# One threshold evaluation of the first attention step moves from VectorE to ScalarE

## The reference, cut to what matters

```
logits = (Xa @ W1) @ W2 @ (Xa @ W3).T
vals   = logits sorted downwards in each row
csum   = cumsum(softmax(vals));  k = sum(csum < 0.9) + 1
A      = softmax(logits with all but the k largest set to -inf)
Xf, Xb, Xa = Rf @ Xf, Rb @ Xb, A @ Xa
Z     += Xf @ U1[s] + Xb @ U2[s] + Xa @ U3[s]
```

## Time and profile before

| what | value |
|---|---|
| median of 3 runs | 2127.34 us (2127.3 to 2127.66) |
| the profiled execution's own time | 2128.81 us |
| its span, first to last instruction | 2127.0 us |
| PE busy | 1859.8 us, 87% of the span |
| DVE busy | 1703.2 us, 80% |
| ACT busy | 1253.2 us, 59% |
| POOL busy | 331.4 us, 16% |
| chain that ended last | DVE 35%, PE 28%, DVE's queue 13%, ACT 13%, issue 10% |

### The profile page before, as it was taken

How to read it: one execution, slowest core, us unless ns; L and a number is a source line. 1 busy time by engine, 2 the same in 40 slices (tenths; PEclk the granted TensorE clock), 3 DMA queues, 4 the chain that set the end, 5 groups by cost and what they waited for, 6 DMA issues and landing times.

```text
span 2127.0 us, 36276 instructions
## 1 busy us (share of the span) xinstructions
PE 1859.8 (87%) x10984; PEld 1378.1 (65%) x10984; DVE 1703.2 (80%) x4231; ACT 1253.2 (59%) x2027; POOL 331.4 (16%) x765
## 2 busy tenths in 40 slices
PE   3999864999999999996846479999999999999997
PEld 2888732777777777775645156666666656666665
DVE  6444557888888888888882489999999999999996
ACT  5222255666666666664521658676777767686752
POOL 4000030000000000000000021313223231313130
PEclk9999967999999999998878689999999999999999
DMA  6899620110111111111003010101101010101022
GB/s 155 200 202 200 169 96 20 47 42 30 42 46 46 46 46 42 30 42 46 22 22 111 5 41 20 40 20 39 34 25 38 21 39 20 39 20 39 20 102 67
DMA packets 60619, 123.87 MB, mean 58 GB/s; under 512 B 13731, under 2 KB 45857, under 8 KB 60448
## 3 DMA queue, kind: packets, MB, share of 16 engines
q1 hardware_dynamic: 50000, 93.58, 13.0%
q0 software_dynamic: 3744, 22.14, 6.8%
q10 hardware_dynamic: 6832, 7.67, 1.0%
HBM read 107.99 MB, written 37.49 MB: 68 GB/s over the span
## 4 chain that ended last, share of the span: by engine, by line
DVE 35%; PE 28%; DVEq 13%; ACT 13%; issue 10%; ACTq 1%; DMA 0%; POOL 0%; POOLq 0%; SPq 0%
DVE scraps L1244 8%; DVE stats L1358 6%; DVE window L1244 5%; PE lg L965 4%; PE bank L1032 3%; PE bank L1011 3%; DVEq L1539 3%; ACT expo L752 3%; ACT turned L771 3%; ACT turned L769 3%; PE bank L986 3%; PE bank L1000 2%; DVE window L1401 2%; DVEq L1405 2%; PE bank L913 2%
## 5 line engine op out<-in xcount | busy, mean ns | idle before, releaser
L1011 PE MATMUL bank<-xcur,probs_t 128*128 128x256 f32 x2704 | 592.2, 379 | 0.0
L1011 PEld LDWEIGHTS bank<-xcur,probs_t 128*128 128x128 f32 x2704 | 509.7, 190 | 67.1
L805 ACT ACTIVATE probs_t<-bank 128x512 f32<-128x512 f32 (+1 forms) x364 | 190.2, 565 | 248.2 <-PE bank L1000 247.0
L1000 PE MATMUL bank<-ident,window 128*128 128x128 f32 x1352 | 200.7, 289 | 131.6 <-DVE kept_inv L1541 117.5
L1000 PEld LDWEIGHTS bank<-ident,window 128*128 128x128 f32 x1352 | 150.4, 145 | 231.2 <-DVE kept_inv L1541 141.3
L986 PE MATMUL bank<-both,s_tile 128*128 128x512 f16 x1352 | 300.1, 379 | 0.0
L1229 DVE TENSOR_SCALAR_CACHE_REDUCE expo<-lg 128x1024 f32 (+1 forms) x208 | 205.0, 1022 | 63.7 <-PE lg L965 53.1
L965 PE MATMUL lg<-k_t,q_tile 64*128 64x512 f32 (+1 forms) x832 | 197.5, 575 | 53.4 <-DVE expo L1229 25.2
L771 ACT ACTIVATE turned<-expo,found 128x3327 uint8<-128x3327 f32 x78 | 239.6, 3072 | 5.3
L769 ACT ACTIVATE turned<-expo,found 128x3327 uint8<-128x3327 f32 x78 | 239.3, 3068 | 3.8
L1358 DVE MAX8 stats<-window 128x8 f32<-128x208 f32 (+1 forms) x780 | 238.8, 384 | 0.0
(11 more groups left out here) (265 smaller groups left out, 2602.0 us busy)
## 6 DMA issues: line engine op xcount, KB each, us to landing
s_tile<-s_scratch SPq DMA_DIRECT2D x52, 832.0 KB, 4.5
expo<-in_adj POOLq DMA_DIRECT2D x25, 831.8 KB, 9.9
s_scratch<-s_tile SPq DMA_DIRECT2D x14, 832.0 KB, 9.5
s_scratch<-probs_t SPq DMA_DIRECT2D x6, 832.0 KB, 9.9
s_scratch<-window SPq DMA_DIRECT2D x6, 832.0 KB, 9.9
q_tile<-q_scratch SPq DMA_DIRECT2D x104, 32.0 KB, 2.1
xa_scratch<-ht ACTq DMA_DIRECT2D x26, 128.0 KB, 1.7
y_scratch<-y_tile SPq DMA_DIRECT2D x26, 128.0 KB, 1.7
```

Source lines behind the costliest of these rows:

```text
L805: A.activation(probs_t[:, k0 * P:(k0 + n) * P], flip_ps[g % 2][:, 0:n * P], ACT.Copy).then_inc(p_moved[s], 1)
L1000: last = T.transpose(flip_ps[g % 2][:, k * P:(k + 1) * P], window[:, (k0 + k) * P:(k0 + k + 1) * P], ident[:, :])
L1011: last = T.matmul(pv_ps[:, 0:D], probs_t[:, k * P:(k + 1) * P], xcur[:, k, :], start=(k == 0), stop=(k == NT - 1))
```

## The change

The constant that says how many evaluations ACT makes in the first attention step goes from 1 to 2. `refine(b, 1)`, which stands behind the scaling of `ht` in ACT's step, now runs there too, and makes the evaluation and the power step that DVE's `evaluate` made. ACT's first evaluation of the first attention step reads only every second column of `expo`, 1664 of 3327, and its constants are adapted to half the mass. DVE takes the final threshold from a new slot of `found` and goes on with `few`. The second attention step computes what it did.

```diff
-UNDER_LEAST = 0x3A831000
-EVALS_SCALAR = (1, 2)
+EVALS_SCALAR = (2, 2)
...
                     A.activation(bias[:, :], slack[b].bitcast(I32), ACT.Copy, scale=SCALAR_POWER[s],
-                                 bias=SCALAR_POWER[s] * (SCALAR_AIM[s] * BITS - 256.0 * BITS))
+                                 bias=SCALAR_POWER[s] * ((SCALAR_AIM[s] - (1 - s)) * BITS - 256.0 * BITS))
...
                 def refine(b, r):
 
-                    if r >= EVALS_SCALAR[s]:
-                        return
-                    A.activation(unused, expo[b][:, 0:N], ACT.Sign, scale=-1.0, bias=tried[b][r], accum_out=signs[:, :])
+                    every = 2 if s == 0 and r == 0 else 1
+                    seen, sample = unused[:, 0:-(-N // every)], expo[b][:, 0:N:every]
+                    A.activation(seen, sample, ACT.Sign, scale=-1.0, bias=tried[b][r], accum_out=signs[:, :])
+                    if s == 0 and r == 1:
+                        A.activation(goal_at[:, :], tried[b][1], ACT.Identity, scale=AIM[0] + GUARD, bias=slack[b])
                     act.drain()
-                    A.activation(unused, expo[b][:, 0:N], ACT.Relu, scale=-1.0, bias=tried[b][r], accum_out=lack[:, :])
-                    A.activation(neg_count[:, :], signs[:, :], ACT.Copy, scale=-0.5, bias=-N / 2.0 - GUARD)
+                    A.activation(seen, sample, ACT.Relu, scale=-1.0, bias=tried[b][r], accum_out=lack[:, :])
+                    A.activation(neg_count[:, :], signs[:, :], ACT.Copy, scale=-0.5, bias=-(-(-N // every)) / 2.0 - GUARD / every)
+                    if s == 0 and r == 1:
+                        A.activation(last_bias[:, :], goal_at.bitcast(I32), ACT.Copy, scale=POWER, bias=-POWER * 256.0 * BITS)
                     act.drain()
...
-                    A.activation(step_by[:, :], minus_under[b][r].bitcast(I32), ACT.Identity, scale=-SCALAR_POWER[s], bias=bias[:, :])
+                    power, by, after = (POWER, last_bias, last_cut[b]) if r == 1 else (SCALAR_POWER[s], bias, tried[b][1])
+                    A.activation(step_by[:, :], minus_under[b][r].bitcast(I32), ACT.Identity, scale=-power, bias=by[:, :])
                     act.drain()
-                    last = A.activation(tried[b][r + 1].bitcast(I32), tried[b][r].bitcast(I32), ACT.Identity, bias=step_by[:, :])
-                    if s == 0:
+                    last = A.activation(after.bitcast(I32), tried[b][r].bitcast(I32), ACT.Identity, bias=step_by[:, :])
+                    if r == 1:
                         last.then_inc(expo_ready[0], 1)
                     act.drain()
...
                     mass_under(b, terms)
                     dve.drain()
-                    if s == 0:
-                        V.scalar_tensor_tensor(out=weight[:, :], in0=under[:, :].bitcast(I32), scalar=float(UNDER_LEAST),
-                                               in1=goal.bitcast(I32), op0=ALU.max, op1=ALU.subtract)
-                        dve.drain()
-                        V.scalar_tensor_tensor(out=cut.bitcast(I32), in0=weight[:, :], scalar=-POWER, in1=cut.bitcast(I32),
-                                               op0=ALU.mult, op1=ALU.add)
-                        dve.drain()
-                        return
...
                     if s == 0:
                         dve.wait_ge(expo_ready[0], t + 1)
-                        V.tensor_copy(cut, found_of(b, 2, 3))
+                        V.tensor_copy(cut, found_of(b, 7, 8))
...
-                    evaluate(b)
                     if s == 1:
+                        evaluate(b)
                         settle(b)
```

More of the change, by code:

```diff
@@ L170, in graph_layers @@
         slack = [found[:, b, 6:7] for b in range(2)]
+        last_cut = [found[:, b, 7:8] for b in range(2)]
         acts = sb("acts", [P, 8])
@@ L177, in graph_layers @@
         neg_count = acts[:, 4:5]
+        goal_at = acts[:, 5:6]
         step_by = acts[:, 6:7]
+        last_bias = acts[:, 7:8]
         mine = sb("mine", [P, 12])
```

## The result

The change makes the kernel slower: 2226.06 us median (2221.2 to 2230.3, 4 runs) against 2127.32 (2127.19 to 2127.66, 4 runs), ratio 1.0463, 95% interval 1.0438 to 1.0489. The forecast was 2210, with 2180 to 2246 as its range. The profiled execution has a span of 2227.3 us, 100.3 more than the one before. The four runs of the changed kernel lie in two pairs, 2229 and 2230 us at a mean granted clock of 0.936 and 2221 and 2223 us at 0.944; the profiled one is of the first pair.

A forecast was written before the change was run, and what follows sets the result against it. A cycle of waits through PE, DVE and ACT bounds the kernel. First step +5.3, 21 periods +84.4, tile 22's retry back to +82.0, next period +86.9, tile 24's retry +83.4: +83 us on 2127.3, 2210 us; range 2180 to 2246.

The forecast's parts named there:

- DVE out of the ring: First attention step: DVE, relieved of 4.38 us per tile, leaves the one-period cycle of waits through PE, DVE and ACT.
- The exponential at S+8.0: ACT's exponential starts 8.0 us after S, the start of a period's timeline, in place of 11.3.
- The halved evaluation hidden: ACT's first evaluation on 1664 columns ends at S+16.9, before the result of A @ Xa at S+18.5: 1.6 us spare.
- Rival C: The stride eats the halving's gain: 1.3 us on 23 periods, +30, 2240 us; chance 0.08.
- The second evaluation, 7.96 us: ACT, between `ht` and the copies PE waits for: a full evaluation's 7.66 us plus two 128 x 1 activations.
- The period without the clock, 31.7: First attention step: 31.7 us per period against 28.68 if PE's clock does not fall behind its new 3.7 us wait.
- The retries: Tiles 22 and 24 retry as before; the first ends at S(22)+19.2, so the shift falls by 7.7 us.
- B: Worse thresholds from the halved first evaluation change retries: two more, 2248 us (chance 0.19); one fewer, 2191 (0.07).
- The prologue and the first step: Before the loop ACT's first threshold comes 5.0 us later, DVE saves 4.38: +0.7; with the first step, +5.3.
- S(1): Start of step 1, forecast at 395.5 against 390.22: +5.3 us.
- The clock, 1.0 us per period: Behind PE's new 3.7 us wait the clock can fall to 0.50; cost 0 to 1.9 us, taken as 1.0.
- S(22): Start of step 22, 21 periods of 32.7 us after S(1) against 28.68: +84.4, together +89.7.

The follow-up runs named there:

- the filled wait: Changed kernel with 29 matmuls of 256 columns without use in PE's wait before the keys and queries; 2192.58 us.
- the halved one: Kernel before with only ACT's first evaluation of the first attention step reading every second column; 2106.99 us, ratio 0.9909.
- the split one: Changed kernel with ACT's second evaluation cut into three pieces placed elsewhere in ACT's step; 2135.10 us, ratio 1.0035 to the kernel before.

## Why the prediction was right, and by how much it was short

The order of the steps as the prediction had them:

- **DVE out of the ring**: right. It waits for the first logits 10.4 us per tile (0.94 before); `few` no longer decides anything.
- **The exponential at S+8.0**: right, 806.22 - 798.42 = 7.80.
- **The halved evaluation hidden**: right, with 1.41 us to spare where 1.6 were forecast, although a pass takes 1.815 us, not 1.61. Rival C (the stride eats the gain) fell.
- **The second evaluation, 7.96 us**: right, 7.93 measured. From `ht` to the Sign 0.37, from its end to the copy 0.69 (0.7).
- **The period without the clock, 31.7**: 31.73, shown by the filled wait.
- **The retries**: the same two tiles. B did not come. The experiment with both evaluations halved shows that this was not safe in general: only the first bears it.
- **The prologue and the first step**: 2.4 us short at S(1). The prologue came 1.0 us earlier than forecast (368.89 for 369.87), the first step took 3.4 more. In step 0 the issue of the store of `ht` takes 1.88 us, in the next steps 0.35; the matmuls behind it are slow as well. Every kernel whose whole second evaluation stands ahead of that store has it (1.70 to 2.07 us), the kernel before, the halved one and the split one don't (0.39 to 0.41); why is open.
- **The clock, 1.0 us per period**: the term that was mis-sized. It is 1.72. I had halved the most that one row allowed (1.9), because the fall need not come each time; it comes in 20 of 24 steps, and where it comes early the keys and queries are slow too, so that a step can lose 2.7 us (34.48). (1.72 - 1.0) x 23 = 16.6 us, about the whole difference between +83 and +98.7. That the time fell into the range is the ring's doing and not luck. That one term makes nearly all of the miss is in part luck, since smaller misses cancel: on the trace, which grew by 100.3 us, the first step is 2.4 over the forecast, the 21 periods to S(22) are 16.5 over it, and 1.4 come back in the retry of tile 22, which ends 17.8 us behind S(22) and not 19.2.

The Trainium skill's "TensorE: Matmul & The Clock Gate", section "HAM oscillation — how this bites in real kernels", says that a loop whose matmuls wait in each round can fall back in each round. The trace agrees, in 20 of 24 steps. The Trainium skill's page "SBUF — State Buffer", section "Specifications (TRN2)", asks for two hits in each 16-byte line for full bandwidth, and a stride of two fp32 gives them. Here the strided pass takes 1.815 us and the contiguous one 1.682, so the measurement decides: nearly free, but 8% dearer.

What the runs leave open: whether the split version could be brought from 29.19 down to 27.83 us, which PE needs by itself, by moving its pieces again; and whether the retries of tiles 22 and 24, 27 us each, could be avoided. Neither was tried.

## What to carry to other kernels

Work taken from a busy engine is worth nothing if it is put, on another engine, between two things that a third is waiting for: look for the place in the receiving engine's stream before counting its busy share, and cut the work if no single place holds it. When a change leaves an engine a new wait inside every round, price the clock behind the wait too, not only the wait. Here 29 matmuls without use in the wait took 33.5 us off the time. And test the parts of a change apart: here one part was worth 20 us and the other cost 140 by itself, and together they cost 99, because the halving is worth 40 where the second evaluation stands.

## What the runs showed of the hardware

- After waits of PE of 3.55 and 3.71 us (5.35 in the first step) the granted clock was below 1.00 during the matmuls with U in 20 of 24 steps, and 0.50 in the stretches shown; after 2.46 to 2.62 us in 14 of 23; after 4.8 to 5.0 us (6.49 in the first step) in all. The waits meant are those before the keys and queries. After 3.00 and 3.06 us, each in one first step, the matmuls were slow, after 2.15 us (the first step with 29 matmuls) they weren't, and after 0.4 to 1.5 us they never were. A slow step costs 1.7 us, and 2.5 to 2.7 where the keys and queries are slow too.
- The falls have a pattern: periods of 31.8, 33.3, 33.5, 34.3 and 34.3 us, and then 31.6, 33.5, 33.3, 34.5 and 34.2, over and over. Whether this is why the runs of the changed kernel lie 9 us apart, and those of the kernel before 0.5 us, was not shown.
- A strided ScalarE pass of 1664 fp32 columns takes 1.815 us, a contiguous one 1.682, and one of 3327 columns 3.07.
